# Weaving the turns of the combine weights among the slot sums, and a kept sum moved to VectorE in every second step

## What is computed

```python
logits = (jnp.einsum('tzd,ed->tze', x, phi_w) + phi_b).reshape(t, z, n, p)   # n = 64 experts, p = 32 slots
D = jax.nn.softmax(logits, axis=3)                 # dispatch weights, over the slots of an expert
C = jax.nn.softmax(logits, axis=2)                 # combine weights, over the experts
X_tilde = jnp.einsum('tznp,tzd->npd', D, x)        # slot sums, over all tokens
...
Y_tilde = jnp.einsum('npd,ndH->npH', X_tilde, expert_w) + expert_b[:, None, :]
Y = jnp.einsum('tznp,npH->tzH', C, Y_tilde)
```

## Time and profile before

| | |
|---|---|
| time, median of 3 runs | 952.89 us (952.81 to 953.38) |
| the profiled execution, its own time | 952.25 us |
| its span, first to last instruction | 950.6 us |
| mean granted TensorE clock | 0.984 of full speed |
| busy in the span: PE, PEld | 905.8 us, 755.3 us |
| busy in the span: DVE, ACT, POOL | 711.5 us, 503.0 us, 527.8 us |

### The profile page before, as it was taken

How to read it: one execution, slowest core, us unless ns; L and a number is a source line. 1 busy time by engine, 2 the same in 40 slices (tenths; PEclk the granted TensorE clock), 3 DMA queues, 4 the chain that set the end, 5 groups by cost and what they waited for, 6 DMA issues and landing times. The chain is left out here.

```text
span 950.6 us, 21865 instructions
## 1 busy us (share of the span) xinstructions
PE 905.8 (95%) x7764; PEld 755.3 (79%) x7764; DVE 711.5 (75%) x1065; ACT 503.0 (53%) x817; POOL 527.8 (56%) x490
## 2 busy tenths in 40 slices
PE   6999999999998968999999999999999989999997
PEld 4877888888887646788888888888887748888886
DVE  1466777777776799999999999999998755555552
ACT  1156555555555365766676676676664353333331
POOL 1257233322232287899999999999998351000100
PEclk9999999999999978999999999999999999999999
DMA  7501111111111153323323223223228995777660
GB/s 251 192 26 43 44 43 43 41 41 43 40 54 30 42 118 79 84 71 96 81 69 99 77 72 99 72 79 100 67 72 309 360 390 193 236 242 239 225 191 18
DMA packets 99973, 111.01 MB, mean 117 GB/s; under 512 B 12228, under 2 KB 91204, under 8 KB 93908
## 3 DMA queue, kind: packets, MB, share of 16 engines
q1 hardware_dynamic: 97760, 106.23, 36.3%
q0 software_dynamic: 1376, 3.70, 1.0%
q10 hardware_dynamic: 788, 0.44, 0.2%
HBM read 72.14 MB, written 38.21 MB: 116 GB/s over the span
## 5 line engine op out<-in xcount | busy, mean ns | idle before, releaser
L1409 PE MATMUL slots_p_sum<-slots_x,slots_disp 128*128 128x256 f32 (+1 forms) x928 | 206.7, 380 | 2.7 <-DVE sums_bias L1039 2.2
L1409 PEld LDWEIGHTS slots_p_sum<-slots_x,slots_disp 128*128 128x128 f32 (+1 forms) x928 | 173.7, 190 | 27.2 <-issue 4.2
L1151 POOL TENSOR_TENSOR slots_comb<-slots_comb,slots_cmax 128x1024 f32<-128x1024 f32 x56 | 108.1, 1949 | 11.3 <-DVE slots_cmax L944 9.9
L1553 PE MATMUL slots_p_turn<-slots_y_parts,slots_hi 128*128 128x512 f32 (+1 forms) x464 | 111.0, 391 | 0.0
L1162 POOL TENSOR_TENSOR slots_comb<-slots_comb,slots_csum 128x2048 f32<-128x2048 f32 x28 | 101.4, 3621 | 7.4 <-DVE slots_csum L921 7.4
L427 POOL TENSOR_TENSOR attend_stack<-attend_rope_a,attend_rope_b 113x128 f32<-113x128 f32 x128 | 54.4, 457 | 90.7 <-DVE attend_rope_b L383 90.7
L1156 POOL TENSOR_TENSOR slots_disp<-slots_disp,slots_dsum 128x2048 f32<-128x2048 f32 x27 | 98.4, 3646 | 0.0
L1553 PEld LDWEIGHTS slots_p_turn<-slots_y_parts,slots_hi 128*128 128x128 f32 (+1 forms) x464 | 84.1, 186 | 18.0 <-issue 0.4
L1197 POOL DMA_DIRECT2D out<-slots_o x29 | 15.9, 548 | 144.1 <-DVE slots_o L1078 144.1
L1442 PE MATMUL slots_logits<-phi_hi,slots_xt_hi 128*128 128x512 f32 x224 | 78.8, 434 | 7.6 <-ACT slots_comb L1261 5.3
L931 DVE TENSOR_TENSOR slots_disp<-slots_logits,slots_dmax 128x512 f32<-128x512 f32 x112 | 77.5, 692 | 4.2 <-PE slots_p_sum L1409 0.3
(11 more groups left out here) (156 smaller groups left out, 1854.9 us busy)
## 6 DMA issues: line engine op xcount, KB each, us to landing
combine_t<-slots_ct SPq DMA_DIRECT2D x224, 128.0 KB, 2.4
slots_comb<-combine_t SPq DMA_DIRECT2D x14, 1024.0 KB, 5.5
slots_ct<-combine_t SPq DMA_DIRECT2D x14, 1024.0 KB, 5.8
expert_w<-wexp SPq DMA_DIRECT2D x8, 1024.0 KB, 9.3
slots_disp<-wexp SPq DMA_DIRECT2D x8, 1024.0 KB, 14.0
h<-attend_h_out SPq DMA_DIRECT2D x32, 113.0 KB
slots_h_t<-h SPq DMA_DIRECT2D x28, 128.0 KB, 2.3
slots_x<-h SPq DMA_DIRECT2D x28, 128.0 KB, 2.1
```

Source lines behind the costliest of these rows:

```text
L1151: nc.gpsimd.tensor_tensor(m, m, cmax[0:rows, shalf(i)].unsqueeze(2).broadcast_to([rows, SLOTS // 2, EXPERTS]), ALU.subtract).then_inc(csub ...
L1409: last = nc.tensor.matmul(p_sum[u % 2][:, i, :], disp[d][part].rearrange("p n s -> p (n s)")[:, 128 * block:128 * block + 128], x[d][part] ...
L1553: return nc.tensor.matmul(p_o[c % 2][0:rows], hi[c % 2][:, e, 0:rows], y_parts[:, e].rearrange("p i c -> p (i c)"), start=e == 0, stop=e = ...
```

## The change

Three things are changed in the middle part, from step 5 on.

1. On TensorE the quarters of turns no longer stand between the banks of logits. The first two stand within the second unit of sums, between its two blocks (`between`), and the last two right behind that unit. The four banks of logits follow in one run. This holds for steps 5 to 28 (in step 28 there are no logits).
2. In the even steps 6 to 26 (11 steps, `by_vector`) the second unit of sums is added to the accumulator by VectorE from PSUM, behind its dispatch sum. ScalarE's copy of that unit and GpSimd's addition fall away.
3. In these steps GpSimd instead adds two columns of one element into a tile `mark`, to raise its counter, and waits for VectorE's addition first.

```diff
--- before.py
+++ after.py
@@ -691,6 +691,7 @@
     comb = [sb(f"comb{i}", [128, SLOTS, EXPERTS]) for i in range(2)]
     e_stats, e_mv, e_rstd = sb("e_stats", [128, EB, 6]), sb("e_mv", [128, EB, 2]), sb("e_rstd", [128, EB])
     e_power = sb("e_power", [128, EB])
+    mark = sb("mark", [128, 1])
     part_sum = [sb(f"part_sum{i}", [128, 2, C]) for i in range(2)]

     logits = pb("logits", [128, EXPERTS, SLOTS])
@@ -789,6 +790,11 @@

         return static(t) and t == LAST

+    def by_vector(t, c, i):
+
+
+        return i == 1 and c % 2 == 0 and not (static(t) and (t <= TG or t == LAST))
+
     def summed_before(t, c):

         return 2 * t - 2 - 2 * ((c - 1) % TG)
@@ -908,8 +914,8 @@

             part = xacc[:, 2 * u:2 * u + 2, :]
             dve.wait_ge(sum_ok, val(s + 1))
-            dve.wait_ge(acc_ok, s)
-            dve.wait_ge(add_ok, s - UNITS + 1)
+            dve.wait_ge(acc_ok, val(s))
+            dve.wait_ge(add_ok, val(s - UNITS + 1))
             nc.vector.tensor_tensor(part, p_sum[u % 2][:], part, ALU.add).then_inc(acc_ok, 1)

         def combine_sum(n, par, rows):
@@ -989,8 +995,9 @@
                 keep_sum(*sums(t, c)[1])
                 return
             dispatch_sum(t, c, rows)
-            for s, u in sums(t, c) if own_sums(t) else []:
-                keep_sum(s, u)
+            for i, (s, u) in enumerate(sums(t, c)):
+                if own_sums(t) or by_vector(t, c, i):
+                    keep_sum(s, u)

         def follow(dve, b):
             lead(dve, b, BATCH - 3, begin)
@@ -1155,7 +1162,12 @@
                     d = disp[c % RING][0:rows]
                     nc.gpsimd.tensor_tensor(d, d, dsum[0:rows, 1].unsqueeze(2).broadcast_to([rows, EXPERTS, SLOTS]),
                                             ALU.mult).then_inc(disp_ok, 1)
-                if units:
+                if units and by_vector(t, c, 1):
+                    s, u = units[1]
+                    pool.wait_ge(acc_ok, val(s + 1))
+                    pool.wait_ge(add_ok, val(s))
+                    nc.gpsimd.tensor_tensor(mark[:], power[:], power[:], ALU.add).then_inc(add_ok, 1)
+                elif units:
                     add_sum(*units[1])
                 pool.wait_ge(crec_ok, val(t + 1))
                 m = comb[c % 2][0:rows]
@@ -1274,7 +1286,7 @@
             if weights:
                 keep_quarter(t - 1, (c + 1) % 2, half(-1), 0)
                 keep_quarter(t - 1, (c + 1) % 2, half(-1), 1)
-                if units and not filling:
+                if units and not filling and not by_vector(t, c, 1):
                     keep_sum(*units[1])
             for i in range(2):
                 if live and not filling:
@@ -1395,10 +1407,10 @@
                                            ident[0:rows, 0:rows])
             last.then_inc(ct_ps_ok, 1)

-        def add_products(u, tiles, newest):
-
-
-            for i in range(2):
+        def add_products(u, tiles, newest, blocks=range(2)):
+
+
+            for i in blocks:
                 e = 2 * u + i
                 for n, (d, rows) in enumerate(tiles):
                     if i == 0 and n == len(tiles) - 1:
@@ -1411,8 +1423,8 @@
                                             x[d][part], start=n == 0, stop=n == len(tiles) - 1)
             return last

-        def multiply_group(t, c):
-            for s, u in sums(t, c):
+        def multiply_group(t, c, between):
+            for n, (s, u) in enumerate(sums(t, c)):

                 group = (c - 1) // TG
                 tiles = [(0, SHORT)] if c <= TG else [(d % RING, 128) for d in range(TG * group - TG + 1, TG * group + 1)]
@@ -1421,7 +1433,12 @@
                     pe.wait_ge(disp_ok, val(done - 1))
                 pe.wait_ge(kept_ok, val(done))
                 wait_for(pe, acc_ok, s - 1)
-                add_products(u, tiles, done).then_inc(sum_ok, 1)
+                if n == 0:
+                    add_products(u, tiles, done).then_inc(sum_ok, 1)
+                else:
+                    add_products(u, tiles, done, [0])
+                    between()
+                    add_products(u, tiles, done, [1]).then_inc(sum_ok, 1)

         def multiply_logits(t, nrows, banks):

@@ -1451,17 +1468,20 @@
             early = static(t) and t <= TG
             if nxt and early:
                 multiply_logits(t, nrows, range(NB))
-            multiply_group(t, c)
-            woven = nxt and not early
+            def first_turns():
+                if not early:
+                    turn_weights(t - 1, c + 1, 0)
+                    turn_weights(t - 1, c + 1, 1)
+
+            multiply_group(t, c, first_turns)
             if not static(t) or t >= 1:
-                turn_weights(t - 1, c + 1, 0)
-                turn_weights(t - 1, c + 1, 1)
-                for q in (2, 3):
-                    if woven:
-                        multiply_logits(t, nrows, [q - 2])
-                    turn_weights(t - 1, c + 1, q)
-            if woven:
-                multiply_logits(t, nrows, [2, 3])
+                if early:
+                    turn_weights(t - 1, c + 1, 0)
+                    turn_weights(t - 1, c + 1, 1)
+                turn_weights(t - 1, c + 1, 2)
+                turn_weights(t - 1, c + 1, 3)
+            if nxt and not early:
+                multiply_logits(t, nrows, range(NB))

         def short_logits(b, columns):
```

## The result

| | median | runs |
|---|---|---|
| before | 952.85 us | 4, 951.95 to 953.38 |
| changed | 959.24 us | 4, 957.81 to 960.29 |
| ratio, 95% interval | 1.0067 | 1.0051 to 1.0083 |

The account below looks back on a forecast made before the run. TensorE was taken to bound the kernel before; after, a ring of 29.37 us per two steps adds 0.23 per step, 5.1 over 22 steps. 952.25 + 5.1 = 957.35, plus 0.6 to the median: 958.0 us, range 951.0 to 961.0.

Parts of the forecast that it names:

- TensorE set the pace before: Middle part before the change: TensorE never waits in 21 steps and sets the step of 14.454 us.
- The wait at the first turns: First turns, moved behind 24 matmuls, reach GpSimd's combine tile early: 1.25 us to spare become 0.48 too few.
- The ring of two steps: Step start to combine tile end, handover, turns to next step: 29.22 us per two steps, 29.37 with VectorE's additions.
- turns ahead of sums: TensorE's run of eight turns directly before slot sums: taken as 0.79 us, 0.88 kept as upper end.
- the row of 0.44 for 4: Profile row behind the middle part: four transposes with sums next take 0.44 us, so 0.88 for eight.
- The handover: GpSimd's signal at the combine tile's end and TensorE's restart: taken as 0.10 us, range 0 to 0.25.
- The size: Total loss: 0.23 us more per step over 22 steps, 5.1 us, giving 958.0 us.
- TensorE alone at 14.38: TensorE's own work per step in the new order, without waits: 14.38 us, 0.07 less than before.
- rival 1: GpSimd was the bound and its relief pays, limited by TensorE at 14.38 per step: 951.3 us; chance 0.14.
- The addition on VectorE: VectorE's addition, 0.55 us ahead of the combine sum: even step's tile ends at 20.29 us, not 20.14.
- 2: Rival: turns nearly free among sums, loads hidden behind matmuls; 14.245 us per step, 948.3 us; chance 0.09.
- 3: Rival: waits cost more than their length because TensorE's granted clock falls; 963 us and more; chance 0.05.

Follow-up runs that it names:

- vector_only: Changed kernel with TensorE's order put back as before the change, VectorE's additions in even steps kept: 954.27 us, ratio 1.0018.
- turns_later: Changed kernel with GpSimd's additions instead of VectorE's and the first eight turns behind 28 of the 32 matmuls, not 24: 953.5 us, ratio 1.0010.
- turns_earlier: Changed kernel with GpSimd's additions instead of VectorE's and the first eight turns behind 16 matmuls, ahead of the whole second unit: 987.7 us, ratio 1.0366.
- keep_later: Changed kernel without VectorE's additions; ScalarE copies the first unit of sums behind the fourth bank of logits, not the second: 953.3 us, ratio 1.0008.
- no_second_add: Changed kernel without VectorE's additions, GpSimd's addition of the second unit also left out in steps 5 to 27: 953.2 us, ratio 1.0013.
- later_vector: Changed kernel with the first turns behind 28 matmuls, not 24, and VectorE's additions kept: 956.56 us, ratio 1.0049.
- weave_only: Changed kernel without VectorE's additions: GpSimd adds every second unit again, TensorE's new order stays: 958.18 us, ratio 1.0073.

## Why the prediction was right

- **TensorE set the pace before**: shown by vector_only. GpSimd's tile comes up to 0.8 us later there and the step stays 14.47, with no wait at the turns.
- **The wait at the first turns**: as forecast by releaser and place, and the loads wait in 19 of 21 steps. The forecast had steps alike, with 0.2 to 0.5 us in each; from step 10 on the turns start 0.4 late in nearly every odd step and hardly late in the even ones. turns_later and turns_earlier move only the place of the turns and give 14.47, 14.68 and 16.07 for 28, 24 and 16 matmuls ahead.
- **The ring of two steps**: forecast 29.22 for the order alone, measured 29.36 (2 x 14.68); forecast 29.37 with the additions, measured 29.52. The terms that were off: turns ahead of sums cost 0.88 (0.92 behind a wait), not 0.79; I had set the row of 0.44 for 4 as the upper end only, and it was the right one. The handover took 0.06, not 0.10, which makes up for the tile, 0.04 later than forecast. keep_later and no_second_add shorten the ring at two different links, and both free TensorE.
- **The size**: forecast +0.23 per step and +5.1 us, measured +0.31, +6.4 us between the medians and +7.4 between the two traces. That 958.0 came so near to 959.24 is in part the luck of the medians: by the steps, the loss was underrated by a quarter.
- **TensorE alone at 14.38**: wrong by 0.08, by the same term. The woven order wins nothing on TensorE even without waits (14.46 to 14.47 against 14.454), so rival 1's 951.3 was never to be had, with whatever relief.
- **The addition on VectorE**: its own tile ended at 20.33 (forecast 20.29). It costs 0.08 per step on top of the order, forecast 0.07. I had the odd steps' tile untouched by it at 20.14; it ends at 606.46 + 3.62 - 589.76 = 20.32, since VectorE's delay carries into the next step. later_vector shows a second way, through ScalarE's copies, that I had not seen.
- **Rivals**: 2 is excluded, turns among sums are dearer, not cheaper. 3 did not occur, the clock stayed at 1.00.
- The Trainium skill's rule ("Perfetto Trace Analysis", section "Identifying the Most-Contended Engine") would have picked GpSimd by its occupancy. The measurements decide otherwise here: 12 us less work for it gained nothing (vector_only), and TensorE, whose loads were busy for 256 of 299 us, was the bound.

## What to carry to other kernels

Where three engines are above 95% busy, look for the one that never waits, and before moving one of its consumers earlier, measure the slack of that consumer's input: 1.25 us were there and 1.7 were taken. A fixed latency through other engines, plus the stretch from the consumer to the next start of that chain, gives the step that results; work it out over as many steps as the chain spans. A late input can be healed by the order on a third engine (one copy on ScalarE here) more cheaply than by moving work between the loaded ones.

## What was not expected of the hardware

A run of 8 transposes costs TensorE 0.88 us ahead of slot sums and 0.79 ahead of logits. A ring of two steps settles into steps of unequal length (14.81 and 14.52 in weave_only) though both steps hold the same work. The first step of the loop's second turn, step 13, is longer in most of the woven kernels: 15.22 us in the changed one, where other odd steps have 14.96, and 14.84 in no_second_add, where others have 14.47. Before, it has 14.45 like the others, though VectorE's combine sum ends 0.2 us later in it (1.81 us into the step, not 1.58) there too: with slack at the turns this costs nothing. Why VectorE is late there no run shows.
